# Two steps of 32 rows in front, one transfer for two tiles, and matmuls of weights before the first step

## The reference, cut to what matters

```python
e = jnp.stack([tbl_0[ids[:, 0]], ..., tbl_31[ids[:, 31]]], axis=1)      # (1024, 32, 16)
for W in (W0, W1, W2):                                                   # W: (32, 32 or 64, 64)
    xk = relu(einsum('bmd,bhd,mhk->bkd', x0, xk, W))
    outs.append(sum(xk, axis=2))
z = concatenate(outs, axis=1)
h = concatenate([z, dense_ctx], axis=1)                                  # (1024, 208)
y = relu(relu(h @ W_top1 + b_top1) @ W_top2 + b_top2) @ W_top3
```

## Time and profile before

| | |
|---|---|
| median of 3 runs | 625.69 us (624.11 to 625.83) |
| the profiled execution, its own time | 622.48 us |
| its span from first to last instruction | 620.7 us |
| first product of DVE | 36.00 us after the start of the span |
| busy share of DVE, PE, POOL | 88%, 91%, 79% |

### The profile page before, as it was taken

The page is one execution under the profiler, slowest core; times in us unless marked ns, Lnnn a source line. Parts: engine busy times, 40 slices in busy tenths (PEclk is TensorE's granted clock), DMA queues, the critical chain, the costliest instruction groups (busy, mean ns, idle before and its releaser), DMA issues.

```text
span 620.7 us, 7817 instructions
## 1 busy us (share of the span) xinstructions
PE 563.6 (91%) x2548; PEld 194.8 (31%) x2548; DVE 546.5 (88%) x321; ACT 308.2 (50%) x1345; POOL 488.3 (79%) x364
## 2 busy tenths in 40 slices
PE   0058997999999999999999999999999999999997
PEld 0012232332322333333333333333333333334354
DVE  0038997999999999999999999999999999999580
ACT  0023735355464745455476736454565736454442
POOL 6765888887889798988888788988888797949360
PEclk9997999999999999999999999999999999999998
DMA  3198878778586868788686858787776858687000
GB/s 99 29 375 315 309 249 310 274 267 295 191 314 210 316 218 311 270 299 295 223 289 215 310 199 313 261 310 274 251 275 213 289 212 311 255 306 271 2 1 0
DMA packets 52852, 150.89 MB, mean 243 GB/s; under 512 B 9830, under 2 KB 17386, under 8 KB 52810
## 3 DMA queue, kind: packets, MB, share of 16 engines
q1 hardware_dynamic: 44608, 148.27, 65.6%
q0 software_dynamic: 8192, 2.11, 2.5%
q10 hardware_dynamic: 10, 0.00, 0.0%
HBM read 147.20 MB, written 3.15 MB: 242 GB/s over the span
## 4 chain that ended last, share of the span: by engine, by line
DVE 33%; PE 29%; DMA 19%; issue 8%; POOL 8%; SPq 2%; ACT 1%; DVEq 0%; POOLq 0%
DVE prod L336 31%; PE y_ps L518 26%; DMA x0bc<-x_rows 14%; POOL emb L291 6%; DMA emb<-table,row_sb 2%; DVE z L364 2%; DMA x_rows<-emb 2%; PE x0g_ps L579 2%; POOL pool_prod L306 2%; SPq L263 1%; PE x0g_ps L584 1%; PE x0g_ps L602 0%; SPq L236 0%; SPq L246 0%; DMA off_sb<-id_offset 0%
## 5 line engine op out<-in xcount | busy, mean ns | idle before, releaser
L336 DVE TENSOR_TENSOR prod<-x0bc,x_ps 128x2048 f32<-128x2048 f32 (+1 forms) x252 | 456.5, 1887 | 13.6 <-ACT x_ps L418 13.1
L518 PE MATMUL y_ps<-prod,w_sb 128*64 128x512 f32 x1640 | 381.2, 598 | 12.2 <-DVE prod L336 12.0
L291 POOL DMA_INDIRECT emb<-table,row_sb x256 | 244.9, 957 | 65.5 <-issue 62.8
L306 POOL TENSOR_TENSOR pool_prod<-x0bc,x_sb 128x1024 f32<-128x1024 f32 x102 | 242.4, 2384 | 48.1 <-ACT x_sb L435 35.0
L518 PEld LDWEIGHTS y_ps<-prod,w_sb 128*64 128x64 f32 x1640 | 115.5, 137 | 253.4 <-issue 214.0
L425 ACT ACTIVATE relu<-y_ps 128x16 f32<-128x16 f32 x480 | 79.6, 296 | 115.3 <-PE y_ps L518 115.3
L418 ACT ACTIVATE x_ps<-y_ps 64x512 f32<-64x512 f32 x128 | 73.0, 570 | 75.4 <-PE y_ps L518 72.8
L518 PE MATMUL y_ps<-pool_prod,w_sb 128*64 128x512 f32 x408 | 104.9, 594 | 2.1 <-POOL pool_prod L306 2.0
L336 DVE TENSOR_TENSOR prod<-x0bc,x0g_ps 128x2048 f32<-128x2048 f32 x32 | 72.8, 2288 | 37.5 <-DMA x0bc<-x_rows 32.4
L435 ACT ACTIVATE x_sb<-relu 64x512 f32<-64x512 f32 x128 | 80.4, 628 | 3.4
L425 ACT ACTIVATION_READ_ACCUMULATOR relu<-y_ps 128x1 f32 x480 | 79.7, 322 | 0.0
(11 more groups left out here) (34 smaller groups left out, 71.0 us busy)
## 6 DMA issues: line engine op xcount, KB each, us to landing
x0bc<-x_rows SPq DMA_DIRECT2D x256, 512.0 KB, 7.0
x0g<-x_rows SPq DMA_DIRECT2D x16, 512.0 KB, 4.7
emb<-table,row_sb POOLq DMA_INDIRECT x256
x_rows<-emb SPq DMA_DIRECT2D x16, 128.0 KB, 2.1
w_sb<-w SPq DMA_DIRECT2D x2, 512.0 KB, 4.7
x_rows<-emb SPq DMA_DIRECT2D x16, 64.0 KB, 2.0
wt_sb<-wt SPq DMA_DIRECT2D x1, 512.0 KB
wt1a_sb<-wt_a SPq DMA_DIRECT2D x1, 256.0 KB
```

The source lines that it names most:

```text
L291: pool.indirect_dma_start(emb[:, turn, DIM * n:DIM * (n + 1)], None, table, bass.IndirectOffsetOnAxis(row_sb[:, at:at + 1], 0)).then_inc(g ...
L306: pool.tensor_tensor(pool_prod[:, n % POOL_RING, 0:width(s)], x0bc[:, slot(s, j), 0:width(s)], x[:, 0:width(s)], ALU.mult).then_inc(pool_p ...
L336: made = dve.tensor_tensor(out, left, right, ALU.mult)
L518: made = pe.matmul(ps[MAPS * h:MAPS * (h + 1), 0:half(s)], w, moving[:, half(s) * h:half(s) * (h + 1)], start=first, stop=final)
```

## The change

`ROWS_OF` becomes 32, 32 and then 15 steps of 64 rows, 17 steps in all; `CHUNKS` covers the same rows as before. In the two short steps POOL makes no product, and DVE all 16 tiles. POOL issues the gathers of steps 0 to 3 (rows 0 to 191) in front of everything, and those of step s + 2 between the products of step s from step 2 on. One transfer fills two tiles that follow each other (`MOVED = 2`): the scratch tensor is laid out by step, so that a field and the next one are neighbours, and a partition reads both at once. `AHEAD` puts the store of step 1 ahead of the last two tile transfers of step 0. The tower's weights are spread over the ends of steps 1, 2 and 3, where they stand behind the next step's `x0g` and ahead of its tiles. PE computes 7 matmuls of weights with weights, whose result is overwritten, from the moment when the first step is in the scratch tensor, and 3 more after layer 0 of step 0.

```diff
-ROWS_OF = [64] * 16
+ROWS_OF = [32, 32] + [64] * 15
+MOVED = 2
-POOL_OF = {STEPS - 2: (5, 4), STEPS - 1: (5, 4)}
+POOL_OF = {0: (0, 0), 1: (0, 0), STEPS - 2: (5, 4), STEPS - 1: (5, 4)}
+GATHERED_FIRST = 4
+AHEAD = {0: (12, 16)}
-CHUNKS = [(0, 4), (4, 8), (8, 12), (12, 15), (15, 16)]
+CHUNKS = [(0, 5), (5, 9), (9, 13), (13, 16), (16, 17)]
+def tile_columns(s, j, count=1):
+    lead = j - j % MOVED
+    at = PAIR * ((TILES * s + lead) % SLOTS) + width(s) * (j - lead)
+    return slice(at, at + width(s) * count)
...
             def load_tiles(s):
-                for j in range(TILES):
+                store_at, load_at = AHEAD.get(s, (TILES, TILES))
+                for j in range(0, TILES + MOVED, MOVED):
+                    if s + 1 < STEPS:
+                        if j == store_at:
+                            store_rows(s + 1)
+                        if j == load_at:
+                            load_x0g(s + 1)
+                    if j == TILES:
+                        break
                     k = TILES * s + j
                     if k >= SLOTS:
-                        wait_free(k - SLOTS)
-                    rows = x0_rows[SHIFT[j]:SHIFT[j] + FIELDS, columns(s)].unsqueeze(1).to_broadcast(
-                        [FIELDS, QUART, width(s)])
-                    sp.dma_start(x0bc[:, slot(s, j), 0:width(s)], rows).then_inc(bc_in[j // GROUP], 16)
+                        wait_free(*divmod(k - SLOTS, TILES))
+                    rows = bass.AP(x0_rows.tensor, rows_at(s) + SHIFT[j] * width(s),
+                                   [[width(s), FIELDS], [0, QUART], [1, MOVED * width(s)]])
+                    sp.dma_start(x0bc[:, tile_columns(s, j, MOVED)], rows).then_inc(bc_in[s % 2][j // MOVED], 16)
...
+            store_rows(0)
+            load_x0g(0)
             for s in range(STEPS):
-                store_rows(s)
-                sp.wait_ge(scratch_out[s % 2], 32 * (s // 2 + 1))
-                load_x0g(s)
                 load_tiles(s)
-                if s == 1:
-                    for dst, src in ((wt1a_sb[:], wt1_a), (wt1b_sb[:], wt1_b), (wt2_sb[:], wt2), (wt3_sb[:], wt3),
-                                     (bt1_sb[:], bt1), (bt2_sb[:], bt2), (zt_b[MAPS:, :], dense_t)):
-                        sp.dma_start(dst, src).then_inc(mlp_in, 16)
+                for dst, src in {1: ((wt1a_sb[:], wt1_a),),
+                                 2: ((wt1b_sb[:], wt1_b), (wt3_sb[:], wt3), (bt1_sb[:], bt1), (bt2_sb[:], bt2)),
+                                 3: ((wt2_sb[:], wt2), (zt_b[MAPS:, :], dense_t))}.get(s, ()):
+                    sp.dma_start(dst, src).then_inc(mlp_in, 16)
...
-            gather(1, 0, GATHERS_OF[1])
+            for s in range(1, GATHERED_FIRST):
+                gather(s, 0, GATHERS_OF[s])
...
-                if x is not None:
+                if x is not None and pool_tiles(s, l + 1):
                     act.wait_ge(relu_done[l], s + 1)
...
+            def keep_going(x, count):
+                for _ in range(count):
+                    pe.matmul(y_bank(x)[0:MAPS, :], w1_sb[:, 0, :], w2_sb[:, 0:HALF // MAPS, :], start=True, stop=True)
...
+            pe.wait_ge(scratch_out[0], 32)
+            keep_going((0, 0), 7)
             layer0(0)
+            keep_going((0, 1), 3)
```

More of the change, by code:

```diff
@@ L140, in summed2_after, with copies_after, rows_at @@
     return FIRST_ROW[min(s + 1, LAST)] // 2 + (1 if s == LAST else 0)
-def slot(s, j):
-    return (TILES * s + j) % SLOTS
+def copies_after(s, l):
+    return 4 * sum(1 for i in range(s + 1) if pool_tiles(i, l + 1))
+def tile_columns(s, j, count=1):
+    lead = j - j % MOVED
+    at = PAIR * ((TILES * s + lead) % SLOTS) + width(s) * (j - lead)
+    return slice(at, at + width(s) * count)
+def rows_at(s):
+    return X0_ROWS * DIM * FIRST_ROW[s]
 def cin_tower_kernel(nc, table, ids, id_offset, dense_t, w0_a, w0_b, w0_sq, w1, w2,
@@ L205, in cin_tower_kernel @@
         x0g_in = sem("x0g_in")
-        bc_in = [sem(f"bc_in{g}") for g in range(TILES // GROUP)]
+        bc_in = [[sem(f"bc_in{i}_{g}") for g in range(TILES // MOVED)] for i in range(2)]
         w0_ready = sem("w0_ready")
@@ L243, in load_x0g @@
                     sp.wait_ge(squared, s)
-                rows = bass.AP(x0_rows.tensor, DIM * FIRST_ROW[s],
-                               [[COLS, FIELDS], [QUART * COLS, QUART], [1, width(s)]])
+                rows = bass.AP(x0_rows.tensor, rows_at(s),
+                               [[width(s), FIELDS], [QUART * width(s), QUART], [1, width(s)]])
                 sp.dma_start(x0g[:, 0:width(s)], rows).then_inc(x0g_in, 16)
[L248 to L254, removed]
@@ L256, in load_tiles, with wait_free @@
-            def load_tiles(s):
-                for j in range(TILES):
+            def wait_free(s, j):
+                own = range(j, j + MOVED)
+                by_pool = [t for t in own if t in pool_tiles(s, 2)]
+                by_vector = [t for t in own if t not in by_pool]
+                if by_pool:
+                    sp.wait_ge(pool_products, pool_before((s, 2)) + pool_tiles(s, 2).index(by_pool[-1]) + 1)
+                if by_vector:
+                    sp.wait_ge(products, before((s, 2)) + by_vector[-1] // GROUP + 1)
@@ L305, in layer @@
                         pool.wait_ge(pool_products_used, n - POOL_RING + 1)
[L306 removed]
+                    pool.tensor_tensor(pool_prod[:, n % POOL_RING, 0:width(s)], x0bc[:, tile_columns(s, j)],
                                        x[:, 0:width(s)], ALU.mult).then_inc(pool_products, 1)
[L308 removed]
+                    if GATHERED_FIRST <= s + 2 < STEPS:
                         gather(s + 2, done, done + gathers[k])
@@ L330, in product @@
                     dve.wait_ge(products_used, n - RING + 1)
-                at, count = slot(s, group[0]), len(group)
+                count = len(group)
                 halves = slice(0, 2) if h is None else slice(h, h + 1)
+                tiles = x0bc[:, tile_columns(s, group[0], count)].rearrange("p (t c) -> p t c", t=count)
                 out, left = (t.rearrange("p t (h c) -> p t h c", h=2)[:, :, halves, :]
-                             for t in (prod[:, n % RING, 0:count, 0:width(s)], x0bc[:, at:at + count, 0:width(s)]))
+                             for t in (prod[:, n % RING, 0:count, 0:width(s)], tiles))
                 right = x[:, halves, 0:half(s)].unsqueeze(1).to_broadcast(list(left.shape))
```

23 lines of the change are left out of this document (10 added, 13 removed).

## The result

The changed kernel took 618.39 us in the median of 4 runs (615.34 to 620.28), the kernel before 625.76 beside it: a ratio of 0.9883, with 95% between 0.9855 and 0.9911. I had said 616.0 (611.5 to 621.0), faster with 0.92. The same kernel once more on another occasion, as an experiment (c1_after), took 615.41 (614.61 to 616.46), 0.9856 of the kernel before (0.9835 to 0.9877). So the time was foretold well. The experiments show that part of the reasoning behind it was not. The two ratios of this one kernel differ by 0.0027; a difference of that size between two groups of runs says nothing.

The account below looks back on a forecast made before the run. DVE was taken to set the pace in the middle, with waits in the head; terms -12.0 + 8.0 - 4.0 - 3.4 + 1.5 = -9.9 us, from the median 625.69 to 615.8, said as 616, 80% in 611.5 to 621.

Parts of the forecast that it names:

- First product, -12.0: Start: eight gathers instead of sixteen and half the bytes bring DVE's first product from 36.00 to 24.0, -12.0 us.
- More work, +8.0: First product to layer 1 of step 2: DVE has 47.0 us of work against 39.1 before, +8.0 us.
- Gaps of the head, -4.0: First steps: DVE's idle time after its first product falls from 8.14 to 4.1 us, -4.0 us.
- Matmuls of weights: First step on PE: the seven cost about what the clock gives, covered by late gathers; PE free at 27.1.
- Wait of 100.73, -3.4: Layer 0 of step 3, formerly step 2: gathers issued in front remove DVE's wait for tiles, -3.4 us.
- Tower weights, +1.5: Step 4: weights standing between x0g and the tiles delay DVE by 1.5 us (0 to 2.5).
- One transfer for two tiles, 0: Tile loads: two tiles per transfer cost nothing, since bytes are the same and the DMA engines full.
- transfers become faster: Rival, 13%: larger pieces lift 384 to some 420 GB/s, short waits of about ten steps go, 612 us.
- Tiles of 1 MB land late: Rival, 5%: at 310 GB/s tiles come 1.2 us late at each of 14 steps, +17, 633 us.
- The head gives it back: Rival, 17%: step 1's gathers land 2 to 3 us later or the seven matmuls end at 31; 619.5 to 621.

Follow-up runs that it names:

- transfers alone: Layout by step and one transfer for two tiles, with the old head (steps, gathers, tower weights) of the kernel before, no matmuls of weights: 624.47 us, 0.9939.
- e6_ahead: Changed kernel with the store of step 2 issued ahead of the last two pairs of tiles of step 1: 614.84 us, 0.9832 of the kernel before.
- f3_head_only_again: Changed kernel's head (short steps, gathers, weights, matmuls) with the old layout and one tile per transfer, run again: 624.25 us, 0.9985 of the kernel before.
- f1_single_again: Changed kernel with its layout by step but one tile per transfer, run again: 619.81 us, 0.9914 of the kernel before.
- e7_pause: Changed kernel with one tile per transfer, and POOL waiting for x1 of step 0 before the gathers of step 3: 617.23 us, 0.9897.
- e3_no_warm: Changed kernel without the ten matmuls of weights, in the first group: 654.19 us, 1.0379 of the kernel before.

## Why the prediction was right, and where it wasn't

By parts, against the kernel before: head alone 0.9985, transfers alone 0.9939 (in the group with the stall, where both it and the kernel beside it are doubtful by some us), layout and head 0.9914, all of it 0.9856 and 0.9883. By the sum of the two alone one would expect 0.992. The times alone therefore hardly show that the parts help each other. The traces do: layer 1 of the step that starts with row 64 begins at 83.24 in the kernel before, at 82.15 with the head alone, and at 76.78 to 78.12 with the head and the new layout.

- **First product, -12.0.** Measured -12.3 (23.69) and -12.2 (23.77). Right, in size and place. With the old layout it is 24.43.
- **More work, +8.0.** From the first product to layer 1 of step 2, c1_after has 53.09 us with 5.77 of waits, 47.3 of work, where I had 47.0. Right.
- **Gaps of the head, -4.0.** 8.14 became 5.77 in c1_after, so -2.4 (0.73, 2.41, 2.01 and 0.62 by its rows), and 7.21 in the first profile, so -0.9 (1.03, 2.88, 2.83 and 0.47). With the old layout it became 10.39, so +2.3: the term was worked out from the old layout's rows, and there it fails in its sign. The gap for ACT is 2.4 to 2.9 instead of 3.6, and that of step 1 is gone, as said. Step 2 was mis-sized: 2.6 to 3.3 us where I had 0.2. Its store went 1.8 us earlier than I let it (47.19), but x0g 2.0 us later (54.02; 52.76 in c1_after), because the store's data land behind tiles; e6_ahead shows it by taking two of these away. The wait at step 2 is what layer 1 of step 2 is late by, 76.78 and 78.12 against 75.1. The 5.70 us from gather to store, the single reading that I had doubted, was no trouble: 28.74 to 29.05 for the first store of step 1, with 29.0 said.
- **Matmuls of weights.** I wrote that they cost about what the clock gives. They ended at 27.1 (26.2 in c1_after), as said; from 32 to 41 the clock is 1.00 with them (c1_after) and 0.81 without, and no layer of DVE is shown to move by it. Right, and they could be left out.
- **Wait of 100.73, -3.4.** 0.18 (c1_after) and 0.72 instead of 3.36. Right for the kernel as it is; with the old layout 2.86 us of it stay.
- **Tower weights, +1.5.** 1.28 and 0.91 us of wait stand at step 4, near the number. With the weights moved away the wait was 2.10, since the store went later. Whether the weights cost what I said isn't settled; moving them gained nothing.
- **One transfer for two tiles, 0.** This is the step that failed: "The bytes are the same. I cost it at nothing: at 384 GB/s and a share of 0.99 the engines are full either way". The earlier trace rows is a window behind the start of a stage. In the first 2.5 us of the windows above the kernel before moves 260 GB/s, and layout and transfer together raise that to 350. What I held at nothing with it was the layout, which I didn't cost as an item at all. The changed kernel (0.9856 and 0.9883) against f3_head_only_again (0.9985) shows that layout and transfer are worth 1.0 to 1.3% in the new head, 6 to 8 us. The layout is 0.7% of it (f1_single_again, 0.9914). The transfer for two tiles by itself is 0.3 to 0.6% by f1_single_again and 0.1 to 0.4% by e7_pause (0.9897, in c1_after's own group, intervals that overlap): for it alone, nothing isn't refuted.
- **Why the total held nonetheless.** I priced every transfer of the new head at 384 GB/s with 3.4 us fixed. In the head the new layout comes near that rate and the old one doesn't (371 and 272 GB/s at step 1): I had counted the gain of the layout inside the head's terms, and given nothing for it in its own. That the two errors cancel is luck; the same sum, made for the head alone, would have said -9.9 too, and that kernel gained 1.1 us. The sum -9.9 (own time 612.6) met 614.62, 2.0 off, of which 1.6 are the gaps of the head. The first profile's 620.28 is 7.7 off, 3.1 by the gaps and 5.1 by the steps of 35.01 us, which the second doesn't have.

The rival "transfers become faster" held in its mechanism, but its price, 4 us below the forecast, was wrong in the same way: it took the forecast for the kernel with slow transfers. "Tiles of 1 MB land late" is refuted in the rate that it needs (408 GB/s in the third window in both profiles, 401 before). "The head gives it back" comes nearest to the kernel with the head alone, though at 624.25 that is above its range.

What stays open: what held ACT and DVE in the first group, why the mean full step is 34.5 to 35.3 us from trace to trace, what the tower's weights cost at step 4, and why rows 64 KB apart land more slowly.

e6_ahead is the fastest median of all (614.84), but not measurably faster than the changed kernel.

## What to carry to other kernels

A rate read from a full stretch doesn't hold for the first microseconds of a stage; read the window in which the wait ends, and price the layout of a read by that. When two edits come together, ask of each term at which state of the other edit it is priced: here the two together gain 7 to 9 us, the head alone 1, and the transfers alone some 4 by a doubtful comparison. And run the changed kernel itself beside its variants: without c1_after I would have blamed three edits for a stall that none of them made.

## What the runs showed of the hardware that I had not expected

- A read of 512 KB into 128 partitions from rows of 4 KB took 4.7 us from issue to landing where the rows lie 64 KB apart, and 3.7 us where they follow on each other, with the same number and size of pieces.
- In one group, all three kernels that issue 48 gathers in a row in front stood in their first step, ACT for 29.35 to 49.36 us. Engines went on 7 to 9 us behind the last gather of the front, and 6 in the kernel with 32 of them; but in e3_no_warm ACT went on at 51.84, with gathers going on until 63. The changed kernel, which has the same head, did not stand on the same chip later, nor did these programs themselves on two others. ACT waited on a semaphore of PE's that, by the profile, had long been due. That gathers hold it back is a guess from four profiles, and no experiment shows it.
- One of eight executions of f1_single_again took 1220.87 us. Nothing in its record tells why.
